# TensorE waits for its own unit two places back, ahead of each shared unit of the last stage

## The reference, cut to what matters

```
x = L0_attn_x                                   # (4, 512, 256)
xn = layernorm(x)
x = x + attention(xn, ...) + ffn(xn, ...)

# in ffn: b*t = 2048 tokens, E = 64 routed experts of width 64, top 4 of each token; S = 2 shared, width 256
sg = silu(einsum('nd,sdh->nsh', flat, swg))
su = einsum('nd,sdh->nsh', flat, swu)
shared = einsum('nsh,shd->nd', sg * su, swd)
return (routed + shared).reshape(b, t, d)
```

## Time and profile before

| | us |
|---|---|
| median of 3 runs | 406.61 |
| lowest and highest | 401.96, 411.38 |
| span of the profiled execution | 407.3 |

### The profile page before, as it was taken

How to read it: one execution, slowest core, us unless ns; L and a number is a source line. 1 busy time by engine, 2 the same in 40 slices (tenths; PEclk the granted TensorE clock), 3 DMA queues, 4 the chain that set the end, 5 groups by cost and what they waited for, 6 DMA issues and landing times.

```text
span 407.3 us, 8670 instructions
## 1 busy us (share of the span) xinstructions
PE 354.1 (87%) x2711; PEld 259.3 (64%) x2711; DVE 248.5 (61%) x717; ACT 189.3 (46%) x359; POOL 257.5 (63%) x522
## 2 busy tenths in 40 slices
PE   6698487988976899899999999999999997989753
PEld 3696355665654556448889999999974544545442
DVE  4668877877876878624554645454444419375676
ACT  3485667686766677533455555555532111010100
POOL 5677986777777665022446566877837757667560
PEclk9969989898999889957999999999999999999969
DMA  8940144444484446545988873577974324434341
GB/s 255 213 109 1 54 131 146 131 146 133 161 241 150 142 146 176 156 141 134 296 263 269 267 249 132 181 244 233 337 252 120 105 85 129 128 94 129 103 129 52
DMA packets 73037, 66.81 MB, mean 164 GB/s; under 512 B 9054, under 2 KB 68702, under 8 KB 72994
## 3 DMA queue, kind: packets, MB, share of 16 engines
q1 hardware_dynamic: 66433, 49.30, 40.8%
q0 software_dynamic: 6144, 16.79, 13.0%
q10 hardware_dynamic: 416, 0.18, 0.2%
HBM read 36.78 MB, written 29.23 MB: 162 GB/s over the span
## 4 chain that ended last, share of the span: by engine, by line
PE 64%; DVE 15%; another core or an unknown queue 8%; issue 5%; ACT 4%; DMA 2%; POOL 1%; SPq 0%; DVEq 0%; ACTq 0%; POOLq 0%
PE bank L650 14%; PE bank L675 8%; PE bank L589 8%; PE bank L515 5%; PE bank L624 4%; PE bank L540 4%; PE bank L609 4%; DVE xall L1092 3%; PE bank L436 3%; PE bank L491 3%; DVE xall L1324 3%; PE bank L417 3%; PE bank L523 2%; PE bank L458 1%
## 5 line engine op out<-in xcount | busy, mean ns | idle before, releaser
L1500 POOL DMA_INDIRECT xs_d<-spare,slot_i x64 | 64.2, 1003 | 29.3 <-PE bank L515 7.5
L1593 POOL DMA_INDIRECT wall<-y_d,y_row x64 | 61.4, 959 | 33.7 <-issue 18.3
L1519 POOL COPY spare<-wall 128x256 f32 x127 | 46.9, 400 | 29.9 <-PE bank L650 18.0
L650 PE MATMUL bank<-xall,spare 128*128 x508 | 64.1, 279 | 0.2
L1284 DVE TENSOR_TENSOR spare<-bank,spare 64x512 f32<-64x512 f32 (+1 forms) x64 | 44.1, 690 | 31.0 <-ACT spare L896 30.1
L650 PEld LDWEIGHTS bank<-xall,spare 128*128 128x128 f32 x508 | 59.4, 192 | 2.8 <-issue 0.7
L589 PE MATMUL bank<-xnT,xall 128*128 128x512 f32 x128 | 57.7, 594 | 0.5 <-issue 0.5
L908 ACT ACTIVATE spare<-bank 128x512 f32<-128x512 f32 (+1 forms) x62 | 33.7, 593 | 29.5 <-PE bank L675 17.9
L847 ACT ACTIVATE xall<-bank 98x1024 bf16<-98x1024 bf16 x32 | 32.7, 1021 | 22.6 <-PE bank L436 14.5
L855 ACT ACTIVATE xall<-bank 128x512 f32<-128x512 f32 x64 | 36.6, 601 | 12.5 <-PE bank L491 7.4
L609 PE MATMUL bank<-xall 128*128 128x256 f32 x128 | 32.0, 400 | 11.6 <-DVE xall L1309 8.3
(11 more groups left out here) (172 smaller groups left out, 656.0 us busy)
## 6 DMA issues: line engine op xcount, KB each, us to landing
y_d<-spare SPq DMA_DIRECT2D x31, 512.0 KB, 4.1
wall<-in_wg SPq DMA_DIRECT2D x16, 256.0 KB, 4.8
wall<-in_wu SPq DMA_DIRECT2D x16, 256.0 KB, 5.0
wdn<-in_wd SPq DMA_DIRECT2D x16, 256.0 KB, 4.5
spare<-xs_d SPq DMA_DIRECT2D x32, 128.0 KB, 2.8
small<-xs_d SPq DMA_DIRECT2D x32, 128.0 KB, 3.3
wall<-in_x SPq DMA_DIRECT2D x4, 512.0 KB, 5.7
base_d<-spare SPq DMA_DIRECT2D x16, 128.0 KB
```

What stands on the lines that cost most here:

```text
L650: ins = pe.matmul(up_bank_of(G)[:, j * P:(j + 1) * P], wcur[i % NW][:, c * 2 * F:(c + 1) * 2 * F], x_half[c][:, bass.ds(o, P)], start=c == ...
L1500: pool.indirect_dma_start(out=xs_d, out_offset=bass.IndirectOffsetOnAxis(ap=slot_i[:, T, k:k + 1], axis=0), in_=x_n[b][:, t, :], in_offset ...
L1519: pool.tensor_copy(wcur[i % NW].rearrange("p (c g f) -> p c g f", c=NC, g=2), wall[:, bass.ds(o, WE)].rearrange("p (g c f) -> p c g f", c= ...
L1593: pool.indirect_dma_start(out=yk[:, T, k, :], out_offset=None, in_=of, in_offset=bass.IndirectOffsetOnAxis(ap=y_row[:, T, k:k + 1], axis=0 ...
```

## The change

Ahead of every unit from p1 and h5 up to p11, TensorE first waits until the unit two places before it in its own order has finished, by the semaphore that this unit adds to. For a hidden unit behind a projection that is the hidden unit before (`shared` at i), for p1 to p9 the projection before (`projected` at T), for h15 it is p9, for p10 h14 and for p11 h15. The constants are NHID = 16, FC = 4. The units p12 to p15 get no such wait, nor do h1 to h4, nor p0. Nothing else is changed.

```diff
@@ -595,13 +595,22 @@
             for kind, i in shared_units():
                 if kind == "hidden":
 
+                    if i == NHID - 1:
+                        pe.wait_ge(s["projected"], NHID - 2 - FC)
+                    elif i > FC:
+                        pe.wait_ge(s["shared"], i)
                     if i > 0:
                         hidden(i, 0)
                         hidden(i, 1)
                 else:
                     T, t = i, i % GT
+
                     if T == 0:
                         pe.wait_ge(s["wshd"], 16)
+                    elif T < NHID - 2 - FC:
+                        pe.wait_ge(s["projected"], T)
+                    elif T < NHID - FC:
+                        pe.wait_ge(s["shared"], T + 1 + FC)
                     if T >= 2:
                         pe.wait_ge(s["based"], T - 1)
```

## The result

| | before | after |
|---|---|---|
| median of 20 runs each, us | 406.52 | 412.39 |
| lowest and highest, us | 400.25, 413.12 | 405.67, 417.82 |
| ratio, 95% interval | | 1.012 (1.008 to 1.017) |
| span of the profiled execution, us | 407.3 | 411.1 |

The changed kernel is slower by 1.2%, where 3.5% faster was forecast. (The ratio is over undisturbed runs alone, so it isn't quite that of the two medians.)

A forecast was written before the change was run, and what follows sets the result against it. Bound: late news of TensorE's finished units. From 319.76, units of 51.6, 3.44 and 10.32, 0.17 and a 1.1 hole reach 386.4; plus 6.45 gives 392.9, 14.4 under the span, so 392.2 from the median; 8-in-10 range 388 to 404 us.

The forecast's parts named there:

- What bounds the kernel: Last stage: news of TensorE's finished units reaches idle readers late, 9.5, 7.8 and 6.4 us at h5, h9, p4.
- What differs between the two kinds is how far TensorE's queue could run ahead: Late versus prompt units: TensorE's full, unbroken queue holds its increments back; four units could stand behind h5, none behind h8.
- TensorE running out of queued work: At 356.94 in h11 TensorE stops for 0.45 us; held increments were said to come in a burst when it runs dry.
- The 22 waits cost nothing when the news is prompt: TensorE's added waits were costed at nothing, the next queued unit giving 1.72 or 3.44 us of cover.
- So I take the late news as gone, all of it: Last stage: with at most two units queued, all late news disappears and TensorE has no hole up to h15.
- the whole gain of 14.4 us: Whole span: forecast saving from 407.3 to 392.9 us, mostly TensorE's holes of 12.05 us less 1.1 remaining.
- The bounds of the waits: The 22 waits without cover: 0.04 us each, 0.9 in all, up to 1.3 us each, 28.6 in all.
- The third rival: Waits hold TensorE because its increment comes only once its queue is dry: 0.45 to 1.3 us each, 402.1 to 420.8; chance 0.14.
- The second rival: Something outside TensorE's queue holds increments, late for ScalarE and VectorE only; waits do nothing, 405 to 408 us; chance 0.11.
- The clock: TensorE's clock should stay at its high level, as after shorter holes of 1.3 to 1.8 us.
- The estimate of four units in the queue: TensorE's queue 64 deep, 8 matmuls and 8 weight loads a unit: run-ahead of four units, matching those behind h5.

The follow-up runs named there:

- e6b: The kernel before with SyncE making the 64 fetches as plain DMAs of the same size, from rows the tokens didn't choose; 388.4 us, before 403.8.
- e1b: The kernel before with no fetch until all 16 hidden units are finished and VectorE's sums last, the repeat of e1; 456.5 us, before 403.8.
- p4: As a run, the kernel before with GpSimd waiting, ahead of tile T's fetches, for hidden unit T+3 in place of T; ratio 1.006.
- r1: The kernel before run again, unchanged, for another profile; 409.2 us.
- e2: The kernel of e1 (fetches after all hidden units, sums last) with the 22 waits of the change added; 459.4 us.
- r3: The changed kernel run once more, unaltered; 409.4 us, ratio 1.012 to the kernel before.
- a4: The changed kernel with each wait for the unit four places back in place of two; ratio 1.014 to the kernel before.
- p3: The kernel before with GpSimd waiting, ahead of tile T's fetches, for hidden unit T+2 in place of T; ratio 1.013.
- e1: The kernel before with no fetch until all 16 hidden units are finished and VectorE's sums behind all additions; 440.2 us, before 370.8.
- e3: The kernel before with only VectorE's order changed, all sums last, fetches as before; 401.0 us, before 370.8.
- e4: The kernel before with GpSimd's 64 indirect fetches taking a quarter of each row, from rows not chosen by the tokens; 373.0 us, before 370.8.
- e6: The kernel before with SyncE making the 64 fetches as plain DMAs of the same size, from rows not chosen; 374.0 us, before 370.8.
- r2: The changed kernel run again as it is; 412.1 us, ratio 1.015 to the kernel before.

## Why the prediction was wrong, point by point

- *What bounds the kernel* was right as far as it was read from rows: the news is late, not the unit, nor the reader. e6b shows the size: with the news in time, TensorE's and VectorE's order as it was and SyncE in GpSimd's place, the one run takes 388.4 us where before takes 403.8, 3.8% less; the forecast had 3.5%.
- *"What differs between the two kinds is how far TensorE's queue could run ahead"* is **the step that failed**. What the runs showed in its place: with one unit behind it in the queue p0's news is 6.0 us late, with all of h1 to p15 in one stream (e1b) nothing is, and the news is late where GpSimd issues indirect DMAs. The step rested on which of TensorE's own waits were met, and GpSimd, which does the same thing throughout the stage, was left out of the comparison. h4 is on time, with GpSimd issuing, and I took that as evidence against GpSimd. But 11 fetches had gone out by the end of h4, 15 by that of h5, and with a pause every four (p4) nothing is late. The same rows fit both readings; the other one would have been seen by asking when each hold ends. Before, the last fetch ahead of the end of the first hold is over at 334.77 - 3.44 = 331.33, and the news comes at 334.53, 3.2 us later; in the two other holds of ScalarE it is 3.0 and 2.9 us. GpSimd stops there because it too waits for `shared`. That its stop is what lets the increments through fits these holds and not all others: p0's news comes at 328.23 after, and p4's at 352.57 before, while GpSimd goes on issuing until 331.8 and 354.5. Nor is a number of fetches in a row the whole rule: h8 is finished six fetches behind a pause both before and in r1, and is on time in the one and 4.0 us late in the other. What releases the increments is open.
- *"TensorE running out of queued work"* as the trigger of the burst was a coincidence of time. In the changed kernel TensorE ran dry at 325.61 and again at 331.82, and h5's news still came only at 335.2, 3.4 us behind the end of GpSimd's last fetch.
- *The 22 waits cost nothing when the news is prompt*: right, shown by e2. *"So I take the late news as gone, all of it"*: wrong, by the step above, and with it the whole gain of 14.4 us.
- *The bounds of the waits* were given as 0.04 to 1.3 us each, the latter from the longest lateness with TensorE "stopped at the next unit". But the increments that were 9.5, 7.8 and 6.4 us late stood in the same rows. The right upper bound for a wait two places back was a late increment less its cover: 9.5 - 1.7 = 7.8 us for h6. Measured were 8.2 us (r3, where h5's news was 9.9 us late), and 2.6 and 3.4 us (the profile after, the first of them ahead of p1). The third rival had the right sign, and that TensorE would wait for just these late increments. Its cause, a queue that has run dry, was not it, and its price came from too narrow a reading: most of the 22 are free, and in each of the three profiles two or three of them cost 1.6 to 8.2 us.
- *The second rival* named the right cause ("something outside TensorE's queue (DMA traffic, GpSimd's fetches)"), then took it that TensorE's own waits would not see it. They do: TensorE sees its increment when ScalarE and VectorE do (335.22 and 335.20).
- *The clock* was taken to stay high, from holes of 1.3 to 1.8 us. The holes that the waits made are longer, and p1 and h6 behind them took 3.5 us more in the profile after, against 2.5 us more of idle time up to h14.
- *That TensorE waits, in place of running ahead*, has its own part in the loss: before, it worked through p1, h6, p2 and h7 while the first hold lasted. Those 10.3 us of queued work (2 x 5.16) were cover, and the change gave part of it away.
- The page "Perfetto Trace Analysis" of the Trainium skill, section "Tensor Engine Instruction", has the engine push the update once PSUM has acknowledged the write. That fits e1b and e6b, where the news is seen within 0.04 us; where it is seen up to 17.0 us late, no run shows whether the push is late or the update's way from there. So the traces don't refute the page, though the prediction took them to. The estimate of four units in the queue, from the page "TensorE: Matmul & The Clock Gate" of the Trainium skill, section "Architectural detail", explained a thing that the queue did not cause.

## What to carry to other kernels

When an increment arrives late, compare the late and the prompt cases against **every** engine's activity, above all one that does a long unbroken series of the same thing, and look at when the news arrives, not only at the engine that sends it. A wait of an engine for its own semaphore was free while the news was prompt (e2); when it is late, the wait costs the lateness less the work queued in between (2.6 us in a4). Run-ahead is the cover for late news, so don't take it away before the cause is known. If the cause can't be removed, ask for fewer increments in time: more PSUM banks, additions that can wait, and fetches that pause where news is due gave 1.8% here.

## What the runs showed of the hardware

- TensorE's semaphore increments can be late by up to 9.9 us at a hidden unit (h5 in r3) and 17.0 at a projection (p12 in p3) while GpSimd issues indirect DMAs at one per 1.25 us. Where GpSimd then stopped, ScalarE saw them 1.3 to 3.5 us after its last issue had ended; others came while it went on (p0 in the profile after, p11 in p3). 64 DMAs with a quarter of the bytes do it as much as with all (41.0 and 41.9 us of holds), the same bytes in plain DMAs from SyncE's queue don't.
- The effect depends on the condition of the chip, or on something else outside the program. Before took 370.8 us beside e1, e3, e4 and e6, with nothing late in any of their four profiles, and medians of 401 to 407 us beside all others. The chip's number was the same, 10, for these four and for r1 and r2. What makes the difference is not known, nor which part of the machine the increments wait in.
- It is not confined to the last stage: h1 starts at 284.4 us in e1 and at 297.0 in e1b, the same program up to there, and the waits of the attention stage, where GpSimd scatters by indirect DMA, end with "remote" only in the second. This was seen, not followed up.
